# A two-batch attention, block and top-k kernel: signed search keys, a regrouped tie step, first picks by tile, and new planner numbers

## The reference

```python
qkv = x @ w_attn + b_attn; q, k, v = jnp.split(qkv, 3, axis=-1)
attn = softmax(q @ k.T / sqrt(C) + causal_mask)
h  = layernorm(x + (attn @ v) @ w_proj + b_proj)
scores = h @ w_router                        # one number per row
top_idx = top_k(scores, 3072)                # 3/4 of the rows of each batch
f  = h.at[top_idx].set(gelu(h[top_idx] @ w_block))
out = layernorm(h + f)
```

## Time and profile before

| | us |
|---|---|
| median of 3 runs | 969.17 (966.97 to 973.5) |
| the profiled execution | 968.08 |
| its span | 966.4 |
| TensorE (PE) busy | 939.0 |
| VectorE (DVE) busy | 769.3 |
| ScalarE (ACT) busy | 635.3 |
| GpSimd (POOL) busy | 273.4 |

### The profile page before, as it was taken

The page is one execution under the profiler, slowest core; times in us unless marked ns, Lnnn a source line. Parts: engine busy times, 40 slices in busy tenths (PEclk is TensorE's granted clock), DMA queues, the critical chain, the costliest instruction groups (busy, mean ns, idle before and its releaser), DMA issues.

```text
span 966.4 us, 15640 instructions
## 1 busy us (share of the span) xinstructions
PE 939.0 (97%) x5078; PEld 805.6 (83%) x5078; DVE 769.3 (80%) x1473; ACT 635.3 (66%) x993; POOL 273.4 (28%) x436
## 2 busy tenths in 40 slices
PE   9999999999999999999999999999999999998991
PEld 7889988888888888888888999888888888887770
DVE  5688996967966786689769999887898778569977
ACT  3566675764864585478555875686688558447985
POOL 3523124253052034512214243323204302211162
PEclk9999999999999999999999999999999999999996
DMA  6535343344253345567433533535778534437935
GB/s 191 175 122 167 115 143 120 120 131 139 80 164 99 102 150 163 157 224 223 155 113 93 194 114 105 164 97 179 243 234 243 178 103 130 120 100 232 314 119 174
DMA packets 89378, 149.53 MB, mean 155 GB/s; under 512 B 7761, under 2 KB 25810, under 8 KB 89298
## 3 DMA queue, kind: packets, MB, share of 16 engines
q1 hardware_dynamic: 89298, 148.54, 48.9%
HBM read 108.66 MB, written 39.85 MB: 154 GB/s over the span
## 4 chain that ended last, share of the span: by engine, by line
PE 94%; DVE 3%; issue 1%; ACT 1%; POOL 0%; ACTq 0%; DVEq 0%; POOLq 0%
PE sbank L515 37%; PE fbank L515 13%; PE obank L1049 11%; PE obank L1051 11%; PE obank L1050 11%; PE obank L1043 2%; PE obank L1045 2%; PE obank L1044 2%; PE fbank L1340 1%; PE fbank L1139 1%; PE mbank L947 1%; PE mbank L970 1%; DVE cmp L1503 1%; PE obank L555 1%; ACT parts L996 0%
## 5 line engine op out<-in xcount | busy, mean ns | idle before, releaser
L515 PE MATMUL sbank<-qT,xT 128*128 128x512 f32 (+2 forms) x1728 | 413.2, 379 | 0.0
L515 PEld LDWEIGHTS sbank<-qT,xT 128*128 128x128 f32 x1728 | 306.4, 189 | 53.0 <-issue 0.3
L872 ACT COPY ring<-sbank 128x512 f32<-128x512 f32 (+3 forms) x288 | 157.6, 549 | 178.2 <-PE sbank L515 126.9
L1001 DVE TENSOR_TENSOR ring_lo<-ring,parts 128x1024 fp32r<-128x1024 f32 (+4 forms) x176 | 179.6, 1027 | 30.9 <-ACT parts L996 30.2
L1049 PE MATMUL obank<-ring_lo,vs 128*128 128x512 f32 x480 | 183.6, 383 | 4.3 <-ACT parts L996 2.6
L1051 PE MATMUL obank<-parts,vs 128*128 128x512 f32 x480 | 181.9, 379 | 0.0
L1050 PE MATMUL obank<-parts,vs 128*128 128x512 f32 x480 | 181.6, 378 | 0.0
L996 ACT CAST parts<-ring 128x1024 fp32r<-128x1024 f32 (+4 forms) x176 | 145.9, 834 | 51.7 <-PE obank L1051 38.9
L982 DVE TENSOR_TENSOR ring<-ring,mbank 128x1024 f32<-128x1024 f32 (+4 forms) x176 | 159.4, 946 | 9.4 <-PE mbank L970 9.4
L989 ACT ACTIVATE ring<-ring 128x1024 f32<-128x1024 f32 (+4 forms) x176 | 143.9, 844 | 24.7 <-DVE ring L982 24.4
L914 DVE TENSOR_TENSOR runmax<-ring,runmax 128x1024 f32<-128x1024 f32 x84 | 107.2, 1276 | 64.7 <-ACT ring L872 64.1
(11 more groups left out here) (222 smaller groups left out, 1203.6 us busy)
## 6 DMA issues: line engine op xcount, KB each, us to landing
vs<-v_scratch SPq DMA_DIRECT2D x288, 256.0 KB, 2.8
v_scratch<-vnew SPq DMA_DIRECT2D x30, 512.0 KB, 3.2
xres<-x SPq DMA_DIRECT2D x16, 512.0 KB, 4.6
out<-tail SPq DMA_DIRECT2D x32, 256.0 KB, 3.2
x_scratch<-xres SPq DMA_DIRECT2D x14, 512.0 KB, 3.0
y_scratch<-yb SPq DMA_DIRECT2D x14, 512.0 KB, 4.6
tail<-x_scratch SPq DMA_DIRECT2D x28, 256.0 KB, 3.5
tail<-y_scratch SPq DMA_DIRECT2D x28, 256.0 KB, 4.3
```

Of the source, the lines that this page charges most:

```text
L515: mm = eng.matmul(o, lhs(lh, k), rhs(rh, k), start=n == 0, stop=n == len(todo) - 1)
L872: act.copy(slot(n)[:, c0:], sbank[n % NSS][:, c0:]).then_inc(a_copy, 1)
L1001: dve.tensor_tensor(slots_lo(ns, c0), slots(ns, c0), f32(hi_of(u)), ALU.subtract).then_inc(v_lo, 1)
```

## The change

**Keys.** `make_keys` makes signed keys (flip the lower 31 bits of negative scores) and takes the top key by masking off the lower 16 bits, as an integer; the shift and the conversion to float go. `compare` and `low_keys` read integer top keys. The table's first threshold starts at the lowest signed value.

**Ties.** `split_ties` gets two more steps that turn the two marks into one number per row; `select` subtracts the sum within the partition, scans, and compares once. Behind the tie sums there are three steps in place of four.

**Picks.** Unit 0 of batch 1 is picked and stored in two halves of one tile (128 KB); the other 15 are as before.

**The planner's numbers.** Entries of `PREFER_US` change (among them "project vhi" 100 and "softmax exp" -4 are dropped, "project xhi" goes from 4 to 15, "final pick" from 30 to -15, "search first" from 60 to -4) and the 2 us of "project xhi" in `MARGIN_US` are dropped; with them the order changes on all five engines. The diff shows two lines of the tables.

```diff
-PREFER_US = {"ffn flo": 100, "final load": 100, "project vhi": 100, "ffn store": 100, "last chain": 60,
+PREFER_US = {"ffn flo": 100, "final load": 100, "ffn store": 100, "last chain": 60, "last router": 60,
...
-MARGIN_US = {"attention_out router": 3, "final scale": 3, "project xhi": 2, "ffn flo": 2, "final_roots": 2,
+MARGIN_US = {"attention_out router": 3, "final scale": 3, "ffn flo": 2, "final_roots": 2, "prepare bias": 1.5,
...
-        top_keys = [keyf[:, 0], mbank[:, 64:64 + NT]]
+        top_keys = [keyi[:, 0], mbank[:, 64:64 + NT].bitcast(I32)]
...
-                signs = (mbank[:, 128:128 + NT].bitcast(I32) if b else keyi[:, 0])[:, k]
-                link(dve, dve.tensor_scalar(signs, bits, 31, -2147483648, ALU.arith_shift_right, ALU.bitwise_or))
+                signs = (mbank[:, 128:128 + NT].bitcast(I32) if b else top_keys[b])[:, k]
+                link(dve, dve.tensor_scalar(signs, bits, 31, 2147483647, ALU.arith_shift_right, ALU.bitwise_and))
                 link(dve, dve.tensor_tensor(keyi[:, 1, k], bits, signs, ALU.bitwise_xor))
-                link(dve, dve.tensor_scalar(keyi[:, 0, k].bitcast(U32), keyi[:, 1, k].bitcast(U32), 16, None,
-                                            ALU.logical_shift_right))
-                link(dve, dve.tensor_scalar(top_keys[b][:, k], keyi[:, 0, k], UPPER, None, ALU.mult))
+                link(dve, dve.tensor_scalar(top_keys[b][:, k], keyi[:, 1, k], -65536, None, ALU.bitwise_and))
...
                 dve.tensor_scalar(gteq[:, 1], deep_keys[b], thr, None, ALU.is_equal).then_inc(v_sel, 1)
 
+                dve.wait_ge(v_sel, 2 * (b + 1))
+                link(dve, dve.scalar_tensor_tensor(out=keyf[:, 2], in0=gteq[:, 0], scalar=2 * UPPER / (UPPER + TOPK),
+                                                   in1=gteq[:, 1], op0=ALU.mult, op1=ALU.add))
+                link(dve, dve.tensor_scalar(keyf[:, 2], keyf[:, 2], UPPER + TOPK, -UPPER, ALU.mult, ALU.add))
...
-                link(dve, dve.tensor_tensor_scan(ahead, ones[:, 0:2 * NT], tot, 0.0, ALU.mult, ALU.add))
-                dve.tensor_tensor(keyf[:, 2], ahead[:, NT - 1:2 * NT - 1], within, ALU.add).then_inc(v_tie, 1)
+                link(dve, dve.tensor_tensor(keyf[:, 2], keyf[:, 2], within, ALU.subtract))
+                dve.tensor_tensor_scan(ahead, ones[:, 0:2 * NT], tot, 0.0, ALU.mult, ALU.add).then_inc(v_tie, 1)
                 dve.wait_ge(v_tie, b + 1)
-                link(dve, dve.scalar_tensor_tensor(out=keyf[:, 0], in0=keyf[:, 2], scalar=float(TOPK), in1=gteq[:, 1],
-                                                   op0=ALU.is_lt, op1=ALU.mult))
-                link(dve, dve.scalar_tensor_tensor(out=left_out if b else sel[:, 1], in0=keyf[:, 0], scalar=0.0,
-                                                   in1=gteq[:, 0], op0=ALU.add, op1=ALU.is_equal))
+                link(dve, dve.tensor_tensor(left_out if b else sel[:, 1], ahead[:, NT - 1:2 * NT - 1], keyf[:, 2],
+                                            ALU.is_ge))
...
-            def pick(dve):
+            def pick(dve, t0, t1):
...
-                dve.copy_predicated(y, left_out[:, 2 * u:2 * u + 2, None].bitcast(U32).broadcast_to([P, 2, C]),
-                                    x1).then_inc(v_pick, 1)
-            at("dve", "final pick", pick)
-            final_store(b, u, y, v_pick, u + 1)
+                i0, n = 2 * u + t0, t1 - t0
+                dve.copy_predicated(y[:, t0:t1], left_out[:, i0:i0 + n, None].bitcast(U32).broadcast_to([P, n, C]),
+                                    x1[:, t0:t1]).then_inc(v_pick, 1)
+
+            def store_half(sp, t):
+                sp.wait_ge(v_pick, t + 1)
+                sp.dma_start(out_rows[b][:, t:t + 1, :], y[:, t:t + 1]).then_inc(st_o[0], 16)
+            if u:
+                at("dve", "final pick", lambda dve: pick(dve, 0, 2))
+                final_store(b, u, y, v_pick, u + 2)
+            else:
+
+                for t in range(2):
+                    at("dve", "final pick", lambda dve, t=t: pick(dve, t, t + 1))
+                    at("sp", "final store", lambda sp, t=t: store_half(sp, t))
...
-            pool.memset(tab[:, 0, 0:1], 0.0).then_inc(g_const, 1)
+            pool.memset(tab[:, 0, 0:1], -32768 * UPPER).then_inc(g_const, 1)
```

## The result

Ten runs of the changed kernel have a median of 974.76 us, and ten of the kernel before, run beside them, 969.54. The ratio is 1.0058 (95% interval 1.0043 to 1.0073). That is +5.2 us where +1.5 was forecast, above the range's upper end of 972.8, though within 1%. The profiled run took 974.53 us, 6.45 more than that of before.

A forecast was written before the change was run, and what follows sets the result against it. TensorE was taken as the bound, with DMA at the end. To the profiled 968.08 us, +1.6 at the start, 0 in the middle and -0.20 + 0.20 - 0.1 at the end gave +1.5, so 969.6 us; range 966.8 to 972.8.

The forecast's parts named there:

- The start, +1.6: Start: group 1's x cast between the qT halves delays WV, so TensorE begins group 0's values 1.6 us later.
- the subtraction from 20.47: Start: the loss taken as WV ready at 22.1 less 20.47, when TensorE took it up before: 1.6 us.
- The second rival, the clock: Start: TensorE's new idle time keeps the clock at half for longer, 1.7 us on top, 971.3 us; 15%.
- one guess: Start, VectorE: WB's cast, beside POOL's low parts, ends at about 18.71; its subtraction, free of POOL, takes 0.69.
- The middle, 0: Middle: reordered steps cost 0 while TensorE never waits; bounds -0.8 us and one wait of 1.6 us.
- The keys, -0.20: End, last search: removing the shift takes one small step ahead of the last round's compare, -0.20 us.
- The third rival: Search's top rounds: VectorE reads integer compare operands at half the pace, +2.5 us, 972.1 us; 5%.
- The first pick, +0.20: End: one step less gives -0.09, but four BN_AGGR now stand ahead of the first pick, +0.20 us together.
- The half pick, -0.1: End: first store goes 0.27 us earlier, 0.2 lost as the queue runs dry; -0.1, between -0.27 and +0.1.
- Faster, 22%: First rival: the load lands early, the start costs nothing and the 0.8 us qT wait goes, 967.2 us; 22%.

The follow-up runs named there:

- m5: Kernel before with one exchange at the start, ScalarE's cast of group 1's x ahead of the second half of qT: 972.49 us, +2.8 against before.
- t4: Kernel before with only the preference and margin of the cast of x set as in the changed kernel: 973.27 us, +3.3 against before.
- q3: The same kernel as m5, run again on another chip: 973.44 us, +5.3 against before.
- m2: Changed kernel with ScalarE's copy that frees the scores' bank put ahead of the normalization near 408 us: 972.95 us, +2.9 against before.
- t3: Changed kernel with only the preference and margin of the cast of x put back to the old values: 968.68 us, -1.2 against before.
- n1: Changed kernel with both ScalarE exchanges, second qT half ahead of the cast and copy ahead of the normalization: 970.49 us, +0.8 against before.
- m3: t3 with the first pick and store of the last batch made whole again: 969.27 us, -0.7 against before.
- p2: Changed kernel with filler products in both TensorE waits at the start, five ahead of the scores, eight ahead of the values: 972.98 us, +3.8 against before.
- q1: The same kernel as p2, run again beside the changed kernel on the same chip: 972.58 us, +4.4 against before.

## Why the prediction was wrong, point by point

- **The start, +1.6.** The mechanism was right, and so was the time at which WV would be used: 22.1 was forecast, 21.5 measured in the profile and 22.2 on average. The step that failed is the subtraction from 20.47. That time is the end of scores that ran at half clock, in one execution; without a stretch there, as in seven of nine profiles of the old order, the values begin at 18.4 to 19.1. So the term was 1.6 where the runs show 3.4. Where the new order too has its stretch over the scores, the landmarks are 1.5 to 1.9 us later than before's (m5, t4, q3): against that one execution the 1.6 holds, but it is not the cost in the median. The second rival, the clock, was given 15%. A stretch does come into nearly every execution (all nine profiles of the new order without a filler ahead of the scores, two of nine in the old); in four of seven it reaches the values, which in the profile of after is worth about 1.5 us, and in three it costs nothing. The argument that waits up to 1.6 us elsewhere left the clock at 1.00 did not carry over to the start. Inside the mechanism one guess was wrong and harmless: WB's cast, begun inside POOL's pair, took 0.42 as when POOL is idle, and the subtraction behind it took 1.66 in place of 0.69.
- **The middle, 0.** This failed. Its upper bound, one wait of up to 1.6 us, is what came: a loss of 1.17 us in the profile, 1.0 on average over nine, and 2.3 by m2's runs, which tell it only to about 2 us. I priced the stretch by TensorE's idle time and never went through ScalarE's new row for a step that waits on POOL with the copy of a scores' bank behind it. By t3 and n1 the other hundreds of moved rows cost nothing that their runs can tell.
- **The keys, -0.20.** Failed: 0. The rounds are no pure chain of VectorE and TensorE; the first count waits for late products. The third rival (integer operands at half pace) is out: a pair takes 0.84 in either kind.
- **The first pick, +0.20.** Right: +0.14 from the marks, in after and in m3.
- **The half pick, -0.1.** Wrong in sign: +0.1 to +0.3, on average 0.2, above its own bound of +0.1. The queue running dry was foreseen, its price was not.
- **Faster, 22%.** No: the load landed with ScalarE waiting 3.74 us for it, and the 0.8 us wait stayed.
- **The rest of the profile's 6.45.** 1.5 is the stretch at 890, put down to the execution. Another 0.44, between the last product with the values and the marks, goes with the load of y: it is issued 5.8 instead of 5.3 us behind the store that it waits for, and ScalarE waits for it ahead of the last rows (2.24 us instead of 1.62). The 5.8 was 4.7 to 6.7 over the twenty profiles; whether that is chance was not tested.
- **The range.** Its upper end came from a rival about the keys that didn't happen, and the terms were set against one execution of before. With the start at 3.4, the copy at 1.0 and the tail at 0.4 the sum is 4.8 us, near the measured 5.2.

What stays open: why the stretch near 890 us comes in a third of the profiles, what about the start brings a stretch there, why three profiles wait again near 524 us, and the 0.5 us of small shifts near 640 and 700 us.

## What to carry to other kernels

When numbers that set an order change, walk each engine's new row and look for a step that waits on a slow engine and has a bank-freeing copy of the bound engine behind it; idle time of the bound engine today says nothing of it. Price a change at a place where the clock moves against several executions, not one: a stretch at half clock may set the time that you subtract from in one, hide behind a wait in the next, and be missing in most. A step saved in a chain is a gain only where the other engine's queue reaches the next link as early, and a store begun earlier only where the next is ready when it ends.

## What the runs showed of the hardware

The granted clock falls to half near the start (17 to 26 us) in all nine profiles with 0.6 to 2.9 us of idle time and no filler ahead of the scores, in two of the nine in which TensorE isn't idle there, and in neither of the two with five more products there, though these are still idle for 0.50 (p2) and 1.18 us (q1). It doesn't fall after the idle 1.4 us at 884 us in before (window 883.5 to 886.9 at 1.00, the next products at 0.23 us apart), and does in after at the same place, 0.1 us before the product that ended the same wait: products 0.43 us apart until 892.6. The Trainium skill (TensorE: Matmul & The Clock Gate, What's actually happening) says that the monitor runs freely, so that the same kernel may meet the step at another place; these runs agree that it varies, with 17 to 31 us at half per run of the kernel before.

A cast and a two-input operation of VectorE meet POOL differently: in after it is 0.42 us for the 128x512 cast begun at 16.83 within POOL's pair (0.41 to 0.43 in all eleven profiles with this start), and 1.66 for the subtraction begun at 17.28, where 0.69 is its time alone. In before the cast at 15.81 took 1.55, so a cast can be held up as well; what decides it was not tried.
